# An LSTM with a mixture of experts behind it: h's low part by one scan over halves of o's tanh, c's tanh and h's high part

## The reference

```
a = xW[t] + prev_h @ Wh                    # (2, 1024)
i, f, o = sigmoid(a[i]), sigmoid(a[f]), sigmoid(a[o]);  g = tanh(a[g])
next_c = f * prev_c + i * g
next_h = o * tanh(next_c)
x = x + h over all steps
x = x + (shared(x) + routed(x)) / 4
```

## Time and profile before

| | us |
|---|---|
| median of 3 runs | 1893.0 (1892.4 to 1893.2) |
| the profiled execution | 1891.8 |
| its span, first to last instruction | 1889.9 |
| PE, DVE, ACT busy | 1809.2, 1544.3, 853.9 |
| mean granted TensorE clock | 0.998 |

### The profile page before, as it was taken

How to read it: one execution, slowest core, us unless ns; L and a number is a source line. 1 busy time by engine, 2 the same in 40 slices (tenths; PEclk the granted TensorE clock), 3 DMA queues, 4 the chain that set the end, 5 groups by cost and what they waited for, 6 DMA issues and landing times.

```text
span 1889.9 us, 111434 instructions
## 1 busy us (share of the span) xinstructions
PE 1809.2 (96%) x45718; PEld 1606.2 (85%) x45718; DVE 1544.3 (82%) x13293; ACT 853.9 (45%) x5545; POOL 121.4 (6%) x403
## 2 busy tenths in 40 slices
PE   8999999999999999999999999999999999999999
PEld 8888888888888888888888888888888888888888
DVE  7888788888888888888888888888888888888885
ACT  4664444444444444444444444444444444444442
POOL 0000000000000000000000000000000000000000
PEclk9999999999999999999999999999999999999999
DMA  6000000000000000000000000000000000000000
GB/s 249 4 4 4 4 7 4 7 4 4 7 4 7 4 4 7 4 6 4 7 4 4 7 4 6 4 4 7 4 7 4 4 6 4 7 4 6 4 4 7
DMA packets 7440, 20.85 MB, mean 11 GB/s; under 512 B 1168, under 2 KB 5648, under 8 KB 6160
## 3 DMA queue, kind: packets, MB, share of 16 engines
q1 hardware_dynamic: 6784, 13.66, 1.9%
q10 hardware_dynamic: 144, 0.07, 0.0%
HBM read 11.63 MB, written 2.10 MB: 7 GB/s over the span
## 4 chain that ended last, share of the span: by engine, by line
DVE 42%; PE 38%; ACT 7%; issue 5%; DVEq 0%
PE gates L816 16%; DVE gates L645 8%; DVE gates L629 7%; DVE addend L641 7%; ACT gates L354 7%; PE gates L834 6%; DVE to L659 6%; PE gates L823 6%; DVE hh L664 3%; DVE gates L660 3%; DVE gates L655 3%; PE acc_lg L860 2%; DVE hid_rt L614 2%; PE gates L842 2%; PE up_rt L854 2%
## 5 line engine op out<-in xcount | busy, mean ns | idle before, releaser
L834 PE MATMUL gates<-hh,wh_lo 128*128 128x24 f16 x8192 | 784.2, 183 | 0.0
L834 PE MATMUL gates<-hh,wh_hi 128*128 128x24 f16 x8192 | 784.2, 183 | 0.0
L834 PEld LDWEIGHTS gates<-hh,wh_hi 128*128 128x128 f16 x8192 | 550.4, 96 | 0.0
L834 PEld LDWEIGHTS gates<-hh,wh_lo 128*128 128x128 f16 x8192 | 549.0, 95 | 0.0
L354 ACT ACTIVATE gates<-gates 128x4 f32<-128x4 f32 x1024 | 161.8, 158 | 835.5 <-DVE gates L629 835.1
L816 PEld LDWEIGHTS gates<-hh,wh_lo 128*128 128x128 f16 x8192 | 273.7, 96 | 275.9 <-DVE hh L664 271.7
L842 PE MATMUL gates<-hh,wh_small 128*128 128x2 f16 x8192 | 489.5, 164 | 0.0
L816 PE MATMUL gates<-hh,wh_lo 128*128 128x24 f16 x8192 | 380.9, 184 | 76.0 <-DVE hh L664 14.6
L629 DVE TENSOR_TENSOR_SCAN gates<-part_fac,gates 128x8 f32<-128x8 f32 x2048 | 295.4, 179 | 163.9 <-PE gates L823 143.0
L823 PE MATMUL gates<-hh,wh_hi 128*128 128x4 f16 (+1 forms) x8192 | 370.1, 171 | 0.0
L842 PEld LDWEIGHTS gates<-hh,wh_small 128*128 128x128 f16 x8192 | 349.8, 96 | 0.0
(11 more groups left out here) (230 smaller groups left out, 2589.7 us busy)
## 6 DMA issues: line engine op xcount, KB each, us to landing
rw_sb<-rw SPq DMA_DIRECT2D x2, 2048.0 KB, 22.7
sw_sb<-sw SPq DMA_DIRECT2D x3, 1024.0 KB, 13.6
x_sb<-xT SPq DMA_DIRECT2D x1, 1920.0 KB, 9.4
outT<-osb SPq DMA_DIRECT2D x15, 128.0 KB, 2.2
wh_sb<-wh SPq DMA_DIRECT2D x2, 512.0 KB, 4.4
wx_sb<-wx SPq DMA_DIRECT2D x1, 1024.0 KB, 6.3
x_sb<-xT SPq DMA_DIRECT2D x1, 128.0 KB, 5.0
outT<-osb SPq DMA_DIRECT2D x2, 64.0 KB, 1.7
```

Source lines behind the costliest of these rows:

```text
L834: mm(copies(q, m, LOW_COPIES)[:, :, :, 1], part, hh[:, c, half:half + 1, :].broadcast_to([P, LOW_COPIES, B]), start=False, stop=False, ski ...
```

## The change

h's low part comes from one scan on DVE that doesn't need the f32 h. The scan computes state = (data0 - state) x factor over five slots per element: a slot times 0 (clears the state), `to_lo` x 1, -1 x 1, `to_hi` x tc, `h_hi` x -4096. That is (1 + to_hi + to_lo) x tc, then 4096 times its difference from `h_hi`, for all 4 columns in one instruction of 20 elements. To have its operands in one fp16 tile, ACT makes o's tanh a second time with fp16 output (`to_hi`), and DVE makes `to_lo` = to - to_hi in the place of `to1`. The factors, with c's tanh among them, lie in o's PSUM bank, so PE writes nothing to o's bank in the first part of the step and o's seeds are copied after the scan. The scale of `h32` changes (no 4096), and PE counts some semaphores up through the tiles instead of taking them back.

```diff
-        tc = beside(I, HC, BESIDE + 64)
+        factor = beside(O, HC * SLOTS, BESIDE).rearrange("p (c e) -> p c e", e=SLOTS)
+        tc = factor[:, :, TO_HI_AT]
...
-        hh = sb("hh", [P, KC, 2, B], F16)
-        h_lo, h_hi = hh[:, :, 0, :], hh[:, :, 1, :]
+        hh = sb("hh", [P, 2, HC, SLOTS], F16)
+        halves = hh.rearrange("p j (c b) e -> p c j b e", b=B)[:, :, :, :, HI_AT]
+        h_hi, to_lo, to_hi = (hh[:, 1, :, j] for j in (HI_AT, TO_LO_AT, TO_HI_AT))
...
                 activation(to[:], o_sum, ACT.Tanh, scale=by_unit).then_inc(s_tanh, 1)
+                activation(to_hi, o_sum, ACT.Tanh, scale=by_unit).then_inc(s_half, 1)
...
+            link(v.memset(factor, 1.0))
+            link(v.memset(factor[:, :, 0], 0.0))
+            link(v.memset(factor[:, :, HI_AT], -LO))
...
                 dve.wait_ge(s_tanh, 3 * n + TO_OF)
-                v.tensor_scalar(to1[:], to[:], 1.0, LO, ALU.add, ALU.mult).then_inc(s_own, 1)
-                v.tensor_copy(parts[O], seeds[:, piece % 2, at, O * HC:I * HC, :].rearrange("p c j -> p (c j)"))
+                dve.wait_ge(s_half, n + 1)
+                v.tensor_tensor(to_lo, to[:], to_hi, ALU.subtract).then_inc(s_own, 1)
 
                 dve.wait_ge(s_tanh, 3 * n + TC_OF)
                 if not final:
-                    v.scalar_tensor_tensor(h_hi, by_batch(to[:]), 1.0, by_batch(tc), ALU.add, ALU.mult).then_inc(s_hhi, 1)
+                    v.scalar_tensor_tensor(h_hi, to[:], 1.0, tc, ALU.add, ALU.mult).then_inc(s_hhi, 1)
 
                 h_now = h32[:, piece % 2, at, :]
-                dve.wait_ge(s_own, 2 * n + 1)
-                v.tensor_tensor(h_now, to1[:], tc, ALU.mult).then_inc(s_own, 1)
+                v.scalar_tensor_tensor(h_now, to[:], 1.0, tc, ALU.add, ALU.mult).then_inc(s_own, 1)
...
+                dve.wait_ge(s_own, 2 * n + 1)
+                dve.wait_ge(s_hhi, n + 2)
+                v.tensor_tensor_scan(hh[:, 0].rearrange("p c e -> p (c e)"), hh[:, 1].rearrange("p c e -> p (c e)"),
+                                     factor.rearrange("p c e -> p (c e)"), 0.0, ALU.subtract, ALU.mult).then_inc(s_hlo, 1)
+                v.tensor_scalar(c_now[:], cs[:, :, 2], 0.5, None, ALU.mult)
+
                 if at == HS - 1:
                     dve.wait_ge(s_staged, tile * PIECES + piece + 2)
-                v.tensor_scalar(c_now[:], cs[:, :, 2], 0.5, None, ALU.mult)
-
-                dve.wait_ge(s_own, 2 * n + 2)
-                v.scalar_tensor_tensor(h_lo, h_hi, -LO, by_batch(h_now), ALU.mult, ALU.add).then_inc(s_hlo, 1)
-
                 v.tensor_copy(parts[I], seeds[:, piece % 2, at, I * HC:GATES, :].rearrange("p c j -> p (c j)")).then_inc(s_seeded, 1)
-
+                v.tensor_copy(parts[O], seeds[:, piece % 2, at, O * HC:I * HC, :].rearrange("p c j -> p (c j)")).then_inc(s_seeded, 1)
...
                 low(F)
                 low(G)
-                one_column(O, blocks[:EARLY // 2])
-
-                pe.wait_ge(s_hlo, s + 1)
+                pe.wait_ge(s_hlo, n + 1)
                 high(F, 1).then_inc(s_mul, 1)
                 high(G, HIGH_COPIES).then_inc(s_mul, 1)
-                if s:
-                    pe.wait_ge(s_seeded, s)
-                elif tile:
-                    take_back(pe, s_seeded, TS)
+                if n:
+                    pe.wait_ge(s_seeded, 2 * n - 1)
                 one_column(I, blocks)
                 and_low(I, 1).then_inc(s_mulio, 1)
-                one_column(O, blocks[EARLY // 2:])
+                if n:
+                    pe.wait_ge(s_seeded, 2 * n)
+                one_column(O, blocks)
                 and_low(O, 1).then_inc(s_mulio, 1)
```

More of the change, by code:

```diff
@@ L26 @@
 APART = 16
-EARLY = 2
 BESIDE = 384
 LO = 2.0 ** 12
+SLOTS = 5
+TO_LO_AT, ONE_AT, TO_HI_AT, HI_AT = 1, 2, 3, 4
 NTOK = B * T
@@ L184, in cond_resid_kernel @@
         to = sb("to", [P, HC])
-        to1 = sb("to1", [P, HC])
         tpart = sb("tpart", [P, NE])
@@ L225, in cond_resid_kernel @@
         s_mul, s_mulio, s_sum, s_tanh = sem("f_g_multiplied"), sem("i_o_multiplied"), sem("f_g_c_summed"), sem("f_o_c_tanh")
-        s_scan, s_seeded = sem("scan_operands_ready"), sem("i_seeds_in_place")
+        s_scan, s_seeded = sem("scan_operands_ready"), sem("i_o_seeds_in_place")
+        s_half = sem("o_tanh_high_part")
         s_piece, s_staged, s_added = sem("piece_of_steps_done"), sem("piece_staged"), sem("h_added_to_x")
@@ L466, in _ @@
             link(v.memset(c_now[:], 0.0))
-            link(v.memset(half_lo, 0.5 / LO))
+            link(v.memset(half_lo, 0.5))
             link(v.memset(hh[:], 0.0))
+            link(v.memset(hh[:, 1, :, ONE_AT], -1.0))
             dve.wait_ge(s_lw0, 16)
@@ L674, in lstm @@
                     return
+                dve.wait_ge(s_own, 2 * n + 1)
[3 more added lines that the diff above has]
+                v.tensor_scalar(c_now[:], cs[:, :, 2], 0.5, None, ALU.mult)
                 if at == HS - 1:
                     dve.wait_ge(s_staged, tile * PIECES + piece + 2)
-                v.tensor_scalar(c_now[:], cs[:, :, 2], 0.5, None, ALU.mult)
-                dve.wait_ge(s_own, 2 * n + 2)
-                v.scalar_tensor_tensor(h_lo, h_hi, -LO, by_batch(h_now), ALU.mult, ALU.add).then_inc(s_hlo, 1)
                 v.tensor_copy(parts[I], seeds[:, piece % 2, at, I * HC:GATES, :].rearrange("p c j -> p (c j)")).then_inc(s_seeded, 1)
+                v.tensor_copy(parts[O], seeds[:, piece % 2, at, O * HC:I * HC, :].rearrange("p c j -> p (c j)")).then_inc(s_seeded, 1)
+                if at == HS - 1:
+                    dve.wait_ge(s_own, 2 * n + 2)
                 if at in (STAGE_AT, HS - 1):
@@ L816, in low @@
                         mm(copies(q, m, n)[:, :, :, 0], wh_lo[:, c, (q * KC + m) * P:(q * KC + m + 1) * P],
-                           hh[:, c, 1:2, :].broadcast_to([P, n, B]), start=False, stop=False, skip_group_check=True)
+                           halves[:, c, 1:2, :].broadcast_to([P, n, B]), start=False, stop=False, skip_group_check=True)
             def high(q, n):
@@ L824, in high @@
                                   wh_hi[:, c, (q * KC + m) * P:(q * KC + m + 1) * P],
-                                  hh[:, c, :, :].rearrange("p (r j) b -> p r b j", r=1).broadcast_to([P, n, B, 2]),
+                                  halves[:, c, :, :].rearrange("p (r j) b -> p r b j", r=1).broadcast_to([P, n, B, 2]),
                                   start=False, stop=True, skip_group_check=True)
@@ L833, in one_column @@
                     for part, half in ((wh_lo[:, c, w], 1), (wh_hi[:, c, w], 1)):
-                        mm(copies(q, m, LOW_COPIES)[:, :, :, 1], part, hh[:, c, half:half + 1, :].broadcast_to([P, LOW_COPIES, B]),
+                        mm(copies(q, m, LOW_COPIES)[:, :, :, 1], part, halves[:, c, half:half + 1, :].broadcast_to([P, LOW_COPIES, B]),
                            start=False, stop=False, skip_group_check=True)
@@ L841, in and_low @@
                         w = slice(((q - O) * KC + m) * P, ((q - O) * KC + m + 1) * P)
-                        last = mm(copies(q, m, n)[:, :, :, 1], wh_small[:, c, w], hh[:, c, 0:1, :].broadcast_to([P, n, B]),
+                        last = mm(copies(q, m, n)[:, :, :, 1], wh_small[:, c, w], halves[:, c, 0:1, :].broadcast_to([P, n, B]),
                                   start=False, stop=True, skip_group_check=True)
@@ L862, in down, with mixture @@
                 return ins
-            def mixture(s, with_xw):
+            def mixture(s, tile):
                 if s == LOGITS:
@@ L917, in mixture @@
                             last.then_inc(s_dn, 1)
-                if with_xw:
+                if tile < NT:
+                    copied = len(XW_FIRST) + (tile - 1) * (MC - MF)
                     if s == 0:
@@ L923, in mixture @@
                         first, final = (c, j) == (0, 0), (c, j) == (KC - 1, len(TERMS) - 1)
-                        if first and m > MF:
-                            pe.wait_ge(s_xwe, m - MF)
+                        if first:
+                            pe.wait_ge(s_xwe, copied + m - MF)
                         of_w, of_x = TERMS[j]
@@ L984, in lstm @@
                 blocks = [(m, c) for m in range(KC) for c in range(KC)]
-                pe.wait_ge(s_hhi, s + 1)
+                n = tile * TS + s
+                pe.wait_ge(s_hhi, n + 1)
                 low(F)
                 low(G)
-                one_column(O, blocks[:EARLY // 2])
-                pe.wait_ge(s_hlo, s + 1)
+                pe.wait_ge(s_hlo, n + 1)
                 high(F, 1).then_inc(s_mul, 1)
                 high(G, HIGH_COPIES).then_inc(s_mul, 1)
-                if s:
-                    pe.wait_ge(s_seeded, s)
-                elif tile:
-                    take_back(pe, s_seeded, TS)
+                if n:
+                    pe.wait_ge(s_seeded, 2 * n - 1)
                 one_column(I, blocks)
                 and_low(I, 1).then_inc(s_mulio, 1)
-                one_column(O, blocks[EARLY // 2:])
```

(8 more changed lines are left out.)

3 lines of the change are left out of this document (removed).

## The result

The changed kernel takes 2088.6 us (median of 4 runs, 2088.0 to 2091.9) against 1892.7 for the kernel before on the same chip: 1.104 times as long, interval 1.102 to 1.105. The direction was forecast, 1918 us with a range up to 1940, but the size is wrong: +196 us where +25 was expected.

What follows compares the result with a forecast made beforehand. The bound was taken to be the length of one recurrence step (1.788 us, 1023 times), not any engine's total. Plain steps +12, DVE's tail +12, splits +1 and memsets +0.5 gave +25.5, so 1918 us, range 1893 to 1940.

Steps and rivals of the forecast that it cites:

- One answer each: Small items: three more memsets +0.5 us; seeds' waits, counter take-backs, POOL signals and c's tanh write at no price.
- the two hand-overs in the sum: Semaphore waits before the scan and before `to_lo` on DVE, each taken as 0.035 us.
- scan's start and length: First half: scan starts 0.195 us behind h's high part and takes 212 ns; 18 ns gained per step.
- o's two more matmuls: On PE, two more matmuls in front of o's last, 2 x 0.025 = 0.05 us later for o's tanh.
- second tanh, its end: On ACT, second tanh starts 0.07 us behind o's first, at 1.06, and ends at 1.23 after L823.
- `to_lo` for L659 and L660: On DVE, `to_lo` starts at 1.265 after L823, high part 0.07 us behind it; copy L660 leaves this chain.
- slack of o's chain: Second half before the change: o's chain comes only 0.01 to 0.02 us behind having decided.
- DVE's tail: Instructions behind the scan delay f's sum in 144 side-job steps by some 0.08 us each: +12 us.
- the fp16 splits: 46 side jobs on DVE, lying between the 128-wide and 256-wide ones in cost: +1 us.
- PE in the first half: PE passes ten matmuls and is free at about 904.35; the low part ends last, by 0.02 us.
- the faster rival: 20-element scan hardly longer than plain DVE instructions (0.16 us), deciding under about 0.19: 1865 us, chance 0.12.
- O's chain decides: Second half after the change: o's chain sets h's high part at 1.338 us, c's at 1.325, by 0.01.

Runs made afterwards that it cites:

- the repair: Changed kernel with single waits, factors moved to i's bank, one block of o's products early again and o's seeds copied before the scan: 1909.1 us.

## Why the prediction was wrong

*What failed.* The step "*One answer each*" and the two hand-overs in the sum. The prediction took 0.035 for every wait in DVE and priced two waits in front of one instruction like one. It named the added wait on the second tanh, and charged what it waits for, but not the wait itself. That is 0.065 in the first half (scan) and 0.07 in the second (`to_lo`), 139 of the 171 us that the forecast was short. No instruction on the recurrence's path of the kernel before had two waits, so no row gave the price. But a sign was there: the mixture has one such place (L606 and L607, in front of L609), and a question for its line shows the second wait as an instruction of its own.

```profile
L607 DVEq EVENT_SEMAPHORE  x120: 21/21/21, 146.1 to 1790.0; - x120
```

With single waits the kernel takes 1931.3 us, inside the range of 1893 to 1940. That is in part luck: a plain step is 1.827 there and not 1.800, by PE's slower reads, and the tail that was to cost 12 us costs nothing.

*What was not considered.* The layout of h's fp16 parts. The prediction read the new tile's shape for DVE and never asked who else reads it. PE does, with the 32 matmuls of a step from the first with both parts to o's last: about 28 ns per step. In the kernel before the layout costs 35 us in all, with the slower low part on DVE.

*Term by term,* in a plain step. The whole is 1.788 to 1.967, +179 ns, where +12 was forecast:

| term | forecast, ns | in the traces and runs, ns |
|---|---|---|
| scan's start and length | -18 | -32: length 196, not 212; start without its extra wait as forecast |
| o's two more matmuls | +50 | +53, by the run with all of o's products late |
| PE's reads | 0 | +28: with the line above, o's tanh comes 1.02 after L834 (1002.14 to 1003.16) instead of 0.94 |
| second tanh, its end | +70 | +76: the fp16 one takes 179, not 173 |
| `to_lo` for L659 and L660 | -77 | -67: spacing to the high part 0.08, not 0.07 |
| slack of o's chain | -14 | -14 |
| separate waits | 0 | +135: 65 and 70 |

The left column adds up to 11, the right one to 179. The steps that are longer than plain ones add 13 us to what they cost before. By chance that is what the forecast had put down for DVE's tail and the fp16 splits (13 us), which didn't come.

*PE in the first half* was misread. The prediction has PE free 0.02 before the low part arrives. But the tenth matmul starts at 904.35 and takes its place of 0.025, so PE is free at 904.375, as L823 starts: in the kernel before the queue of ten and the low part end together. In the changed kernel this did no harm, since two of the ten had left; it is what the repair ran into. Two slips in the sums (0.52 for the tail, where it says 0.525, and 1.335 for the high part, where it says 1.338) change nothing.

*The scan* is the term that went better: the slope of 2.75 ns per element was taken from two scans in f32 that write to PSUM, and at 20 elements, written as fp16 to SBUF, it gives 16 ns too many. The page of the changed kernel:

```profile
L685 DVE TENSOR_TENSOR_SCAN hh<-hh,gates 128x20 f16<-128x20 f16 x1023 | 200.1, 196 | 45.6 <-DVE h L675 4.9
```

It is 6 ns above the 12-element one, and 184 in the version with single waits and an early block. The Trainium skill's half throughput (page "DVE: opcode table, instruction layouts, handler registers and perf-mode slots", section "Datapath and trigger behaviour"), from which 207 was estimated, is nearer, and too long as well: for eight more elements that estimate has 17 ns, and the trace 6. The point of the faster rival, a scan under 0.19, was thus almost met, and the kernel is still slower by 10%.

*DVE's tail* in side-job steps, +12 us, did not come, though the delay itself did. In a step with the 256-wide product (L622 here) f's sum starts 0.89 behind the high part, where a plain step has 0.81, and yet the next high part is 1.97 later as always:

```profile
207.74 0.16 DVE L672 SCALAR_TENSOR_TENSOR hh<-to,gates 128x4 f16<-128x4 f32 x1
...
208.30 0.41 DVE L622 TENSOR_TENSOR hid_rt<-ge,up_sh 128x256 f32<-128x256 f32 x1
208.63 0.24 DVE L637 TENSOR_TENSOR_SCAN gates<-part_fac,gates 128x8 f32<-128x8 f32 x2
...
209.71 0.16 DVE L672 SCALAR_TENSOR_TENSOR hh<-to,gates 128x4 f16<-128x4 f32 x1
```

The prediction took the 1.02 from f's sum to the next high part as needed. In the changed kernel's plain steps it is 1.16 (1002.44 to 1003.60), since o's chain is longer, and a sum that is 0.08 late hides in that. The step that failed is the sum it was compared with, not the queue.

*O's chain decides*, with c's tanh no longer last: right. That o's matmuls and the second tanh each cost on the path is shown by the two runs, at 31 and 65 us. The chances (0.76 for slower) had the sign; the range had no case for a cost that no row of before prices.

## What to carry to other kernels

Count the waits in front of each instruction on a latency-bound path. If it needs two, write the one that is released last first, or let both producers count on one semaphore; a wait that stands alone and is released last cost 65 to 70 ns here, twice per step 7% of the kernel. When a tile's layout changes for one engine, list its other readers and writers; here the strided tile cost 1.9% alone. Before making one input of an engine sooner, look what else that engine has queued in front of its use: here PE's own ten matmuls ended together with the low part. And a saving of one instruction's latency is only as good as its whole set of new operands: here two fp16 halves, a second tanh, a moved block of matmuls.

## What the runs showed of the hardware

- Two waits ahead of one DVE instruction: free if the one written first is the last to be released (1895.0 against 1892.8 us), 65 to 70 ns if it is the second (1969.5): the instruction starts 0.10 after its producer's end instead of 0.035.
- Two more separate waits per step in DVE's queue bring occasional longer steps, by 0.27 us in the mean; with single waits the kernel is 16 to 19 us shorter.
- A 28-column matmul whose moving operand has its innermost neighbours 20 elements of fp16 apart took 189 ns against 174, and 188 with the innermost 5 apart and the next 20. One-part matmuls with neighbours 10 apart took 166 against 164, and followed each other by 26.6 ns against 25.0.
- The low part on DVE, reading and writing fp16 at every fifth element, took 173 ns against 162; a tanh with fp16 output took 179 on ACT at every fifth element and 168 into a dense tile.
- A scan of 20 elements over fp16 in SBUF with factors in PSUM takes 196 or 184 ns; 12 elements take 190. Its length says little about its element count at this size.
- c's tanh took 187 ns instead of 158 when it started 0.05 behind another tanh; it wasn't on the path here.
